# Attention with a constant column for the valid flags, and another order of GpSimd's large operations and of the first rearranging copies

## The chip, the cores and the metric

The kernel runs on one core of a Trainium2 chip. The metric is the device time of one execution in microseconds (us), the median of several runs; a profiled execution gives the trace from which all rows below are taken. Engines are named as in the profile: PE is TensorE's matmuls and PEld its weight loads, DVE is VectorE, ACT is ScalarE, POOL is GpSimd, SP is SyncE, which issues most of the DMAs.

## The reference, cut to what matters

```python
B, S, D, M, I = 32, 128, 512, 128, 2048
x = x + tanh(g_xattn[0]) * xattn(layernorm(x), ctx, mask)     # mask true: this key counts
x = x + tanh(g_ffn[0]) * ffn(layernorm(x), w_gate, w_up, w_down)

def xattn(h, mem, mask):
    scores = einsum('bsd,bmd->bsm', h, mem) / sqrt(D)
    scores = where(mask[:, None, :], scores, -1e30)
    readout = einsum('bsm,bmd->bsd', softmax(scores), mem)
    return where(any(mask, -1)[:, None, None], readout, 0)    # no valid key: nothing is added

def ffn(h, w_gate, w_up, w_down):
    h = silu(h @ w_gate) * (h @ w_up)
    return keep_2_largest_of_4(h) @ w_down
```

## The kernel before, in words

The work has two stages. The **attention stage** goes through the 32 batch rows b, each a tile of 128 tokens by 512, in 39 software-pipelined **slots** n (SLOTS = 32 + 7). Every engine runs its own loop over n in a fixed order, and in slot n it does different steps for different rows: PE transposes ctx and the normed x of row n-1, makes the scores of row n-2, transposes x1n of row n-7, multiplies probabilities by ctx for row n-4 and transposes the probabilities of row n-3. ACT copies the two transposes of row n-1, takes the exponential of row n-3, norms x of row n (xn), copies x1n's transpose of row n-7, and copies the transposed probabilities of row n-3 while it scales them. DVE's slot begins with the two small bn_aggr (L892 for row n-6, L896 for row n+1), and goes on with the masked scores (L909) and their minimum (L912) of row n-3, x1 of row n-5 (L924, attention plus residual), x1n of row n-6 (L930, the second layernorm, a tensor_scalar), and the bn_stats of x1 (L935, row n-5) and of x (L943, row n+2). POOL adds eps to the variances (L529), raises them and the softmax sum to their powers (L535, 128x3), and makes the shift of xn (L538, L542). DVE's x1n waits for that power, and POOL's addition waits for DVE's bn_aggr. In the text, the **start of slot n** is the start of L892 in it (for the first slots, L896).

Four kinds of work are laid into slots by hand, by the tables at the top of the file, for the feed-forward stage that follows:
- the mask: one DMA of 32 x 128 flags to all partitions, queued on SP behind the rows x and ctx of b = 0 and 1, with the two gates; POOL turns it into 0 or 1e30 (L548, four pieces of 1024, in slots 1, 2 and 3 by CONVERT), and DVE reduces it to one valid flag per row (L900, four operations), which with the gate scales the probabilities;
- the first weights: SP loads w_raw pieces (PIECE_AT, and two ahead of the slots), ACT rearranges them to w_blk ("spread", L290, SPREAD_AT), DVE makes sums of blocks (w_sum, SUM_AT), and ACT and POOL split each of 7 products' weights into a high and a low part (w_high on ACT, w_low L306 on POOL one slot later, W0_AT), which SP stores;
- the first x blocks, split in the same way (x_high on ACT, x_low L347 on POOL one slot later, X0_AT, 14 of them, with 8 DVE sums x_sum);
- in the last three slots PE already makes the first products of the feed-forward stage (product, L1231, L1233, L1235).

SP's loop loads x and ctx of row n+4 in slot n, once x1 of row n-5 is done (nine buffers each), stores x1 of row n-5, and stores 1 MB of transposed x1n every fourth slot. The order on DVE and on POOL around the change is (POOL's base, power and shift stand ahead of these lines):

```python
                if n in SUM_AT:
                    for u, i in SUM_AT[n]:
                        w_sum(dve, u, i)
                if n + 1 in X0_AT:
                    x_sum(dve, 0, *X0_AT[n + 1])
...
                if n - 1 in W0_AT:
                    w_low(pool, nc.gpsimd, 0, W0_AT[n - 1])
                if n - 1 in X0_AT:
                    x_low(pool, nc.gpsimd, 0, *X0_AT[n - 1])
```

The **feed-forward stage** runs 16 steps of two units of 14 products and 8 output tiles; it takes from the last slots to the end.

Of the kernel before, what the change touches and what calls it, by code (L numbers as in the profile page):

```python
# [5 lines left out]
F32 = mybir.dt.float32  # L6
# [24 lines left out]
BIG = 1e30  # L31
RING = 8
# [15 lines left out]
CONVERT = {1: (0,), 2: (1,), 3: (2, 3)}  # L48
# [52 lines left out]
def flamingo_gated(nc, x, ctx, mask, g_xattn, g_ffn, w_gate, w_up, w_down, out):  # L101
# [9 lines left out]
    with whole:  # L111
# [36 lines left out]
        neg_scores = sb("neg_scores", [P, 2, M], F32, 4)  # L148
# [9 lines left out]
        bn_mv = sb("bn_mv", [P, RING, 2, 2], F32, 4)  # L158
# [5 lines left out]
        eps = sb("eps", [P, 2], F32, 4)  # L164
# [3 lines left out]
        valid = sb("valid", [P, B], F32, 4)  # L168
        gate_valid = sb("gate_valid", [P, B], F32, 4)
        ident = sb("ident", [P, P], F32, 4)  # L170
        x_blk1 = sb("x_blk1", [P, 4, HALF], F32, 4)
        mask_in = x1nT[:, 0, 0:2].rearrange("p c n -> p (c n)").bitcast(U8)

# [29 lines left out]
        gates_loaded, mask_loaded, mask_neg_done = sem("gates_loaded"), sem("mask_loaded"), sem("mask_neg_done")  # L203
        neg_mean_done, shift_done = sem("neg_mean_done"), sem("shift_done")
        base_set = sem("base_set")
        ident_set, ident_done, half_done = sem("ident_set"), sem("ident_done"), sem("half_done")
        gates_done, valid_done, gate_valid_done = sem("gates_done"), sem("valid_done"), sem("gate_valid_done")
# [168 lines left out]
        def _(sp):  # L376
# [52 lines left out]
            load_w_piece(sp, nc.sync, 0, 0)  # L429
            load_w_piece(sp, nc.sync, 0, 1)  # L430
# [75 lines left out]
        def _(pool):  # L506
            nc.gpsimd.memset(base3[:], 1.0).then_inc(base_set, 1)
            nc.gpsimd.memset(eps[:], EPS)
            nc.gpsimd.memset(minus_one[:], -1.0)
            nc.gpsimd.memset(exponent3[:], -0.5).then_inc(half_done, 1)  # L510
            pool.wait_ge(half_done, 1)
            nc.gpsimd.memset(exponent3[:, 2:3], -1.0).then_inc(half_done, 1)
            nc.gpsimd.memset(ident[:], 0.0).then_inc(ident_set, 1)
# [3 lines left out]
            pool.wait_ge(half_done, 2)  # L517
            pool.wait_ge(base_set, 1)

            for n in range(-1, SLOTS - 1):  # L520
# [6 lines left out]
                if first or second:  # L527
                    part_v = slice(0 if first else 1, 2 if second else 1)
                    nc.gpsimd.tensor_tensor(base3[:, k, part_v], bn_mv[:, k, part_v, 1], eps[:, part_v],  # L529
                                            ALU.add).then_inc(base_done, 1)  # L530
                    pool.wait_ge(base_done, n + 2)
                if third:
                    pool.wait_ge(probs_done, n - 3)
                part_p = slice(0 if first else 1, 3 if third else 2 if second else 1)
                nc.gpsimd.tensor_tensor(power3[:, k, part_p], base3[:, k, part_p], exponent3[:, part_p],  # L535
                                        ALU.pow).then_inc(power_done, 1)
                if first:
                    nc.gpsimd.tensor_tensor(neg_mean[:, k:k + 1], bn_mv[:, k, 0, 0:1], minus_one[:],  # L538
# [4 lines left out]
                                            ALU.mult).then_inc(shift_done, 1)  # L543
                if n in CONVERT:
                    pool.wait_ge(mask_loaded, 16)
                    for at_m in CONVERT[n]:
                        part_m = slice(at_m * RING * M, (at_m + 1) * RING * M)
                        nc.gpsimd.tensor_scalar(mask_neg[:, part_m], mask_in[:, part_m], -BIG, BIG, ALU.mult,  # L548
                                                ALU.add).then_inc(mask_neg_done, 1)
# [43 lines left out]
        def _(act):  # L593
# [5 lines left out]
            for n in range(SLOTS):  # L599
# [8 lines left out]
                if 0 <= b < B:  # L608
                    act.wait_ge(neg_max_done, b + 1)
                    wait(act, pT_done, b - 1)  # L610
                    nc.scalar.activation(probs[:, b % 2], neg_scores[:, b % 2], ACT.Exp, bias=neg_max[:, b % RING:b % RING + 1],
                                         scale=-1.0, accum_out=base3[:, (b + 4) % RING, 2:3]).then_inc(probs_done, 1)
# [8 lines left out]
                if 0 <= b < B:  # L621
                    h = b // TILES
                    if b == 0:
                        act.wait_ge(mask_neg_done, 4)
                        act.wait_ge(valid_done, 4)
# [6 lines left out]
                    else:  # L632
                        if b % TILES == 0:
# [5 lines left out]
                if 0 <= b < B:  # L639
                    act.wait_ge(pT_done, b + 1)  # L640
                    wait(act, av_done, b - 1)
                    if b == 0:
                        act.wait_ge(gate_valid_done, 1)
                    nc.scalar.activation(probsT[:, b % 2], ps_pT[:, 0:P], ACT.Identity,
                                         scale=gate_valid[:, b:b + 1]).then_inc(pT_copied, 1)
                if n == 1:
# [240 lines left out]
        def _(dve):  # L887
            for n in range(-2, SLOTS):
                b = n - 6
                if 0 <= b < B:  # L890
                    dve.wait_ge(bn2_done, b + 1)
                    nc.vector.bn_aggr(bn_mv[:, n % RING, 1], bn6[:, 1, b % 2]).then_inc(stats2_done, 1)  # L892
# [443 lines left out]
```

## Time and profile before

| | us |
|---|---|
| median of 3 runs | 1117.73 (1117.38 to 1119.66) |
| the profiled execution | 1116.94 |
| its span, first to last instruction | 1115.1 |
| attention stage, to PE's first product | 134 |
| PE busy over the span | 1082.4 |

The profiled execution is 1.84 longer than its span and 0.79 shorter than the median. PE is busy 97% of the span, but in the attention stage PE's rows are overlapping short matmuls; there the time per slot has to be read from the starts of the slots and from the chain that ended last.

### The profile page before, as it was taken

How to read it: one execution, taken by the hardware profiler on the slowest of the kernel's cores; microseconds unless marked ns; L12 is line 12 of the kernel's file. 1: busy time of each engine (PE TensorE's matmuls, PEld its weight loads, DVE VectorE, ACT ScalarE, POOL GpSimd, SP SyncE). 2: the span in 40 equal slices, each digit the busy share in tenths (PEclk: the TensorE clock that was granted, in tenths of full speed). 3: DMA queues.
4: the chain of work that ended last, by engine and by line, in shares of the span. 5: the costliest groups of instructions: out<-in, count | busy, mean ns of one | idle time of the engine just before them, and what ended most of it. 6: DMA issues, size and time to landing. Idle time of an engine off the chain costs nothing.

```text
span 1115.1 us, 15146 instructions
## 1 busy us (share of the span) xinstructions
PE 1082.4 (97%) x4960; PEld 880.0 (79%) x4960; DVE 809.6 (73%) x1400; ACT 620.1 (56%) x1132; POOL 210.6 (19%) x328
## 2 busy tenths in 40 slices
PE   6998799999999999999999999999999999999998
PEld 5776587777878888888888888888888888888886
DVE  6999969879897757576775767675757565565765
ACT  5999678566765544454544444454445454443452
POOL 5576610121210111111111111001111111111111
PEclk9999999999999999999999999999999999999999
DMA  7899586798869977797779777888878666767726
GB/s 273 295 349 329 202 326 226 219 289 280 257 226 354 356 196 198 187 257 185 202 197 374 182 202 200 237 235 208 231 230 274 151 153 156 189 159 189 199 29 137
DMA packets 89533, 254.75 MB, mean 228 GB/s; under 512 B 9072, under 2 KB 9072, under 8 KB 85104
## 3 DMA queue, kind: packets, MB, share of 16 engines
q1 hardware_dynamic: 67856, 205.55, 52.2%
q0 software_dynamic: 21600, 48.24, 26.1%
q8 instruction: 40, 0.66, 0.2%
q14 instruction: 37, 0.30, 0.1%
HBM read 154.14 MB, written 99.61 MB: 228 GB/s over the span
## 4 chain that ended last, share of the span: by engine, by line
PE 73%; DVE 14%; ACT 4%; issue 4%; POOL 2%; DMA 2%; SPq 0%; DVEq 0%; ACTq 0%; POOLq 0%
PE ps_y L1302 9%; PE ps_a L1231 9%; PE ps_a L1233 9%; PE ps_a L1235 9%; PE ps_y L1304 9%; PE ps_y L1303 9%; PE ps_d L1233 4%; PE ps_d L1231 4%; PE ps_d L1235 4%; PE ps_c L1233 2%; PE ps_c L1231 2%; PE ps_c L1235 2%; DVE beats L980 2%; DMA w_raw<-in_L_ffn_w_up 1%; DVE x1n L930 1%
## 5 line engine op out<-in xcount | busy, mean ns | idle before, releaser
L569 POOL DMA_DIRECT2D out_rows<-y_out x124 | 107.1, 871 | 735.2 <-ACT y_out L717 712.7
L1231 PE MATMUL ps_a<-xm,w_ring 128*128 128x512 f32 x512 | 200.7, 392 | 3.6 <-ACT cp L597 3.3
L1233 PE MATMUL ps_a<-xm,w_ring 128*128 128x512 f32 x512 | 200.3, 391 | 0.0
L1235 PE MATMUL ps_a<-xm,w_ring 128*128 128x512 f32 x512 | 200.2, 391 | 0.0
L1302 PE MATMUL ps_y<-dn,h_hi 128*128 128x512 f32 x480 | 188.9, 394 | 4.4 <-ACT y_out L717 3.3
L1304 PE MATMUL ps_y<-dn,h_lo 128*128 128x512 f32 x480 | 187.4, 390 | 0.0
L1303 PE MATMUL ps_y<-dn,h_hi 128*128 128x512 f32 x480 | 187.0, 390 | 0.0
L717 ACT ACTIVATE y_out<-ps_y,ffn_gate 128x512 f32<-128x512 f32 x124 | 84.8, 686 | 158.4 <-PE ps_y L1304 158.3
L694 ACT ACTIVATE h_hi<-hidden 128x512 fp32r<-128x512 f32 x128 | 73.6, 626 | 107.0 <-DVE hidden L1006 107.0
L980 DVE TENSOR_TENSOR beats<-h_abs 128x512 bf16<-128x512 f32 x186 | 117.7, 684 | 1.3 <-ACT h_abs L687 1.3
L1231 PEld LDWEIGHTS ps_a<-xm,w_ring 128*128 128x128 f32 x512 | 96.4, 188 | 26.2 <-issue 5.2
L1235 PEld LDWEIGHTS ps_a<-xm,w_ring 128*128 128x128 f32 x512 | 96.5, 188 | 20.4
L1233 PEld LDWEIGHTS ps_a<-xm,w_ring 128*128 128x128 f32 x512 | 96.4, 188 | 20.0
L1302 PEld LDWEIGHTS ps_y<-dn,h_hi 128*128 128x128 f32 x480 | 90.1, 188 | 27.4 <-ACT y_out L717 7.4
L948 DVE TENSOR_TENSOR cp<-ps_c,cp 128x512 f32<-128x512 f32 x64 | 43.6, 689 | 93.7 <-PE ps_c L1235 93.7
L1304 PEld LDWEIGHTS ps_y<-dn,h_lo 128*128 128x128 f32 x480 | 90.1, 188 | 19.4
L1303 PEld LDWEIGHTS ps_y<-dn,h_hi 128*128 128x128 f32 x480 | 90.2, 188 | 18.7
L1231 PE MATMUL ps_d<-xm,w_ring 128*128 128x512 f32 x256 | 99.7, 390 | 0.5 <-ACT hidden L670 0.5
L1235 PE MATMUL ps_d<-xm,w_ring 128*128 128x512 f32 x256 | 99.6, 389 | 0.0
L1233 PE MATMUL ps_d<-xm,w_ring 128*128 128x512 f32 x256 | 99.6, 389 | 0.0
L954 DVE TENSOR_TENSOR hidden<-ps_a,hidden 128x512 f32<-128x512 f32 x64 | 43.8, 690 | 65.2 <-PE ps_a L1235 62.9
L687 ACT ACTIVATE h_abs<-hidden 128x512 f32<-128x512 f32 x124 | 74.1, 625 | 28.3 <-DVE hidden L972 28.3
(109 smaller groups left out, 1876.6 us busy)
## 6 DMA issues: line engine op xcount, KB each, us to landing
w_ring<-w_scratch SPq DMA_DIRECT2D x147, 512.0 KB, 4.5
out_rows<-y_out POOLq DMA_DIRECT2D x124, 256.0 KB, 4.3
w_scratch<-w_ring SPq DMA_DIRECT2D x56, 512.0 KB, 4.7
xm_scratch<-x_out SPq DMA_DIRECT2D x42, 512.0 KB, 5.4
xm<-xm_scratch SPq DMA_DIRECT2D x21, 1024.0 KB, 8.4
w_raw<-in_L_ffn_w_down SPq DMA_DIRECT2D x9, 1024.0 KB, 7.8
x_in<-in_x SPq DMA_DIRECT2D x32, 256.0 KB, 4.7
ctx_in<-in_ctx SPq DMA_DIRECT2D x32, 256.0 KB, 5.0
```

The lines of the kernel that those rows point to most:

```text
L569: nc.gpsimd.dma_start(out[RING * (n // (2 * TILES * QS)) + TILES * ORDER[order] + n % TILES], y_out[:, n % 4], accum_op=ALU.add).then_inc( ...
L687: nc.scalar.activation(abs_of(s, order)[:, j], hidden[:, h, j], ACT.Abs).then_inc(abs_done, 1)
L694: nc.scalar.activation(h_hi[:, h, j], hidden[:, h, j], ACT.Copy).then_inc(h_hi_done, 1)
L717: nc.scalar.activation(y_out[:, n % 4], ps_y[n % 2][:], ACT.Identity, scale=ffn_gate[:]).then_inc(y_copied, 1)
L954: nc.vector.tensor_tensor(hidden[:, 1, j], ps_a[e][:], hidden[:, 1, j], ALU.add).then_inc(c22_done[e], 1)
L980: nc.vector.tensor_tensor(beats[:, PAIR[i, j]], abs_of(s, order)[:, i], abs_of(s, order)[:, j], ALU.is_ge).then_inc(beats_done, 1)
L1231: nc.tensor.matmul(to, w_ring[:, k, e, 0, c], xm[:, k, 0, c], start=begins and c == 0, stop=False, skip_group_check=not begins)
L1233: nc.tensor.matmul(to, w_ring[:, k, e, 0, c], xm[:, k, 1, c], start=False, stop=False, skip_group_check=not begins)
L1235: last = nc.tensor.matmul(to, w_ring[:, k, e, 1, c], xm[:, k, 0, c], start=False, stop=c == 1, skip_group_check=not begins)
L1302: nc.tensor.matmul(to, h_hi[:, h, j, at], right[:, 0, j], start=at_j == 0, stop=False)
L1303: nc.tensor.matmul(to, h_hi[:, h, j, at], right[:, 1, j], start=False, stop=False)
L1304: last = nc.tensor.matmul(to, h_lo[:, h, j, at], right[:, 0, j], start=False, stop=at_j == GROUP - 1)
```

## The change

- The scores get one more column that is always FEW = 0.9e30. The minimum over 129 columns is then a real score if any key is valid, and 0.9e30 if none is, so that all exponentials are 0; the softmax sum gets LEAST = 1e-30 added before its reciprocal. DVE's four valid reduces (L900) and the product with the gate (L939) are gone, and ACT scales by the gate alone. The softmax sum is now written into `stats` beside the variances, and one POOL addition (base) covers all three values; it therefore waits for the exponential, as the power did.
- The mask comes in four DMAs: piece 0 and the gates behind the rows of b = 2, piece 1 behind b = 7, the others behind b = 8. The two weight pieces ahead of the slots go out behind b = 6. CONVERT has its four operations in slots 1, 5, 7 and 10.
- POOL waits for x1n of its slot before CONVERT, w_low and x_low.
- The tables move: spreads of unit 0 to slots 5, 6, 8 and 9 (were 3, 6, 9, 12), of unit 1 to 19, 20, 35, 36 (20, 23, 26, 29); sums one per slot in 11 to 14 and 37, 38 (13 twice, 14, 15, 30 twice); loads to match; x_high from 21 to 34 without a gap (19 to 25 and 29 to 35), x_low one slot later, and x_sum in the slot of x_high, not one ahead: slots 24 to 27 and 31 to 34 (were 21 to 24 and 31 to 34).
- The two tanh are in slot 2 of ACT (were slot 1), and ACT's wait for the mask pieces in slot 23 (was 7).

```diff
-CONVERT = {1: (0,), 2: (1,), 3: (2, 3)}
+CONVERT = {1: 0, 5: 1, 7: 2, 10: 3}
...
-PIECE_AT = {4: (0, 2), 7: (0, 3), 10: (1, 0), 13: (1, 1), 21: (1, 2), 24: (1, 3), 27: (2, 0), 30: (2, 1)}
-SPREAD_AT = {3: (0, 0), 6: (0, 1), 9: (0, 2), 12: (0, 3), 20: (1, 0), 23: (1, 1), 26: (1, 2), 29: (1, 3)}
-SUM_AT = {13: ((0, 0), (0, 1)), 14: ((0, 2),), 15: ((0, 3),), 30: ((1, 0), (1, 1))}
-W0_AT = {5: 0, 8: 1, 14: 2, 15: 3, 16: 4, 17: 5, 18: 6}
-X0_AT = {19 + i: (0, i) for i in range(7)} | {29 + i: (1, i) for i in range(7)}
+PIECE_AT = {6: (0, 2), 7: (0, 3), 10: (1, 0), 11: (1, 1), 20: (1, 2), 21: (1, 3), 36: (2, 0), 37: (2, 1)}
+SPREAD_AT = {5: (0, 0), 6: (0, 1), 8: (0, 2), 9: (0, 3), 19: (1, 0), 20: (1, 1), 35: (1, 2), 36: (1, 3)}
+SUM_AT = {11: (0, 0), 12: (0, 1), 13: (0, 2), 14: (0, 3), 37: (1, 0), 38: (1, 1)}
+W0_AT = {7: 0, 10: 1, 14: 2, 15: 3, 16: 4, 17: 5, 18: 6}
+X0_AT = {21 + i: (0, i) for i in range(7)} | {28 + i: (1, i) for i in range(7)}
...
+            def load_mask(m):
+                at_m = slice(m * GROUP_M, (m + 1) * GROUP_M)
+                sp.dma_start(mask_in[:, at_m], mask.rearrange("b m -> (b m)")[at_m].rearrange("(a n) -> a n", a=1)
+                             .to_broadcast([P, GROUP_M])).then_inc(mask_loaded[m], 16)
...
-                if b == 1:
-                    sp.dma_start(mask_in, mask.rearrange("b m -> (b m)").rearrange("(a n) -> a n", a=1)
-                                 .to_broadcast([P, B * M])).then_inc(mask_loaded, 16)
+                if b == 6:
+                    load_w_piece(sp, nc.sync, 0, 0)
+                    load_w_piece(sp, nc.sync, 0, 1)
+                if b == 7:
+                    load_mask(1)
+                if b == 2:
+                    load_mask(0)
...
+            nc.gpsimd.memset(neg_scores[:, :, M:M + 1], FEW).then_inc(few_set, 1)
...
-                if first or second:
-                    part_v = slice(0 if first else 1, 2 if second else 1)
-                    nc.gpsimd.tensor_tensor(base3[:, k, part_v], bn_mv[:, k, part_v, 1], eps[:, part_v],
-                                            ALU.add).then_inc(base_done, 1)
-                    pool.wait_ge(base_done, n + 2)
+                part_p = slice(0 if first else 1, 3 if third else 2 if second else 1)
                 if third:
                     pool.wait_ge(probs_done, n - 3)
-                part_p = slice(0 if first else 1, 3 if third else 2 if second else 1)
+                nc.gpsimd.tensor_tensor(base3[:, k, part_p], stats[:, k, part_p, 1], least[:, part_p],
+                                        ALU.add).then_inc(base_done, 1)
+                pool.wait_ge(base_done, n + 2)
...
+                if second:
+                    pool.wait_ge(x1n_done, n - 5)
                 if n in CONVERT:
...
-                if n in CONVERT:
-                    dve.wait_ge(mask_loaded, 16)
-                    for m in CONVERT[n]:
-                        nc.vector.tensor_reduce(valid[:, m * RING:(m + 1) * RING],
...
-                    nc.vector.scalar_tensor_tensor(neg_scores[:, b % 2], ps_sc[b % 2][:, 0:M], -SCALE,
+                    nc.vector.scalar_tensor_tensor(neg_scores[:, b % 2, 0:M], ps_sc[b % 2][:, 0:M], -SCALE,
                                                    mask_neg[:, b * M:b * M + M], ALU.mult, ALU.add).then_inc(neg_scores_done, 1)
+                    if b == 0:
+                        dve.wait_ge(few_set, 1)
...
-                if n + 1 in X0_AT:
-                    x_sum(dve, 0, *X0_AT[n + 1])
+                if n in X0_AT:
+                    x_sum(dve, 0, *X0_AT[n])
```

## Rows read from the trace of the kernel before

**Rows 1.** The page: busy time, share of the span and instructions of each engine.
```profile
PE 1082.4 (97%) x4960; PEld 880.0 (79%) x4960; DVE 809.6 (73%) x1400; ACT 620.1 (56%) x1132; POOL 210.6 (19%) x328
```

**Rows 2.** Windows: stretch, length, busy time by engine (count), PE clock, DMA share, GB/s.
```profile
28.64:48.19 19.55, 19.30 (x138) 15.66 (x138) 18.67 (x49) 19.55 (x50) 11.20 (x26) 1.00 0.97 339
...
78.60:96.89 18.29, 15.62 (x103) 11.31 (x102) 18.15 (x37) 16.75 (x37) 10.68 (x21) 1.00 0.95 355
...
134.16:174.00 39.84, 39.84 (x182) 32.96 (x183) 29.44 (x47) 29.84 (x50) 6.48 (x10) 1.00 0.86 322
```

**Rows 3.** The chain that ended last, attention stage: start, length, what.
```profile
80.58 1.45 DVE x1n L930
...
119.04 1.25 POOL xm L347
...
134.16 0.66 PE ps_d L1266 x4
```

**Rows 4.** One line's instructions, L930: duration in ns, min/median/max.
```profile
L930 DVE TENSOR_SCALAR x1n<-x,bn_mv,power x32: 535/546/1550, 27.0 to 139.2; 128x512 f32<-128x512 f32 x32
```

**Rows 5.** The same view for L943.
```profile
L943 DVE BATCH_NORM_STATS2 bn<-x_in x32: 669/676/694, 3.5 to 112.6; 128x6 f32<-128x512 f32 x32
```

**Rows 6.** Timeline, slots 20 and 21, POOL's large operations: start, length, engine, line.
```profile
77.49 1.27 POOL L347 TENSOR_TENSOR xm<-x_blk,xm 128x512 fp32r<-128x512 f32 x1
...
80.48 1.27 POOL L347 TENSOR_TENSOR xm<-x_blk,xm 128x512 fp32r<-128x512 f32 x1
```

**Rows 7.** Timeline of DVE: starts of slots 13 to 16, and the first sum.
```profile
48.19 0.16 DVE L892 BATCH_NORM_AGGREGATE bn_mv<-bn 128x2 f32<-128x6 f32 x1
...
50.43 0.69 DVE L312 TENSOR_TENSOR w_blk<-w_blk 128x512 f32<-128x512 f32 x1 [1.43 <-ACT w_blk L290]
...
54.08 0.16 DVE L892 BATCH_NORM_AGGREGATE bn_mv<-bn 128x2 f32<-128x6 f32 x1
...
57.71 0.16 DVE L892 BATCH_NORM_AGGREGATE bn_mv<-bn 128x2 f32<-128x6 f32 x1
...
62.26 0.16 DVE L892 BATCH_NORM_AGGREGATE bn_mv<-bn 128x2 f32<-128x6 f32 x1
```

**Rows 8.** Timeline of DVE: starts of slots 30 to 32, x1n of slot 31.
```profile
113.22 0.17 DVE L892 BATCH_NORM_AGGREGATE bn_mv<-bn 128x2 f32<-128x6 f32 x1
...
117.82 0.18 DVE L892 BATCH_NORM_AGGREGATE bn_mv<-bn 128x2 f32<-128x6 f32 x1
...
119.69 0.89 DVE L930 TENSOR_SCALAR x1n<-x,bn_mv,power 128x512 f32<-128x512 f32 x1
...
121.22 0.18 DVE L892 BATCH_NORM_AGGREGATE bn_mv<-bn 128x2 f32<-128x6 f32 x1
```

**Rows 9.** Timeline, first 29 us; in brackets the idle time before and its releaser.
```profile
10.48 0.69 DVE L943 BATCH_NORM_STATS2 bn<-x_in 128x6 f32<-128x512 f32 x1 [3.37 <-DMA x_in<-in_x]
...
14.59 1.91 PE L1258 MATMUL ps_c<-ctxT,xnT 128*128 128x128 f32 x8
...
15.15 2.31 DVE L900 TENSOR_REDUCE valid<-x1nT 128x8 f32<-128x1024 uint8 x2
...
17.38 0.28 DVE L909 SCALAR_TENSOR_TENSOR neg_scores<-ps_c,mask_neg 128x128 f32<-128x128 f32 x1
...
20.57 1.12 ACT L290 ACTIVATE w_blk<-w_raw 128x512 f32<-128x512 f32 x1 [1.11 <-DMA w_raw<-in_L_ffn_w_gate]
...
28.64 0.17 DVE L892 BATCH_NORM_AGGREGATE bn_mv<-bn 128x2 f32<-128x6 f32 x1
```

**Rows 10.** Timeline: ACT's exponential of slot 10, DVE's x1 of slot 12.
```profile
41.45 0.55 ACT L611 ACTIVATE probs<-neg_scores,neg_max 128x128 f32<-128x128 f32 x1
...
45.79 0.75 DVE L924 SCALAR_TENSOR_TENSOR x<-ps_y,power,x_in 128x512 f32<-128x512 f32 x1
```

**Rows 11.** DMA issues from 73.6 to 74.5: KB each, us to landing.
```profile
x_in<-in_x SPq DMA_DIRECT2D x1, 256.0 KB, 7.1
```

**Rows 12.** Windows, 70 to 90 us, columns as in the second group.
```profile
70.00:90.00 20.00, 18.26 (x124) 13.56 (x123) 19.43 (x45) 18.93 (x45) 14.91 (x29) 1.00 1.03 391
```

More of the change, by code:

```diff
@@ L31 @@
 BIG = 1e30
+FEW = 0.9e30
+LEAST = 1e-30
 RING = 8
@@ L202, in flamingo_gated @@
         ctx_in_loaded = [sem(f"ctx_in_loaded{k}") for k in range(INPUTS)]
-        gates_loaded, mask_loaded, mask_neg_done = sem("gates_loaded"), sem("mask_loaded"), sem("mask_neg_done")
+        gates_loaded, mask_neg_done = sem("gates_loaded"), sem("mask_neg_done")
+        mask_loaded = [sem(f"mask_loaded{k}") for k in range(B // RING)]
         neg_mean_done, shift_done = sem("neg_mean_done"), sem("shift_done")
-        base_set = sem("base_set")
+        stats_set, few_set = sem("stats_set"), sem("few_set")
         ident_set, ident_done, half_done = sem("ident_set"), sem("ident_done"), sem("half_done")
-        gates_done, valid_done, gate_valid_done = sem("gates_done"), sem("valid_done"), sem("gate_valid_done")
+        gates_done = sem("gates_done")
         bn1_done, stats1_done, bn2_done, stats2_done = (
@@ L543, in _ @@
                                             ALU.mult).then_inc(shift_done, 1)
+                if second:
+                    pool.wait_ge(x1n_done, n - 5)
                 if n in CONVERT:
[L545 to L549, printed above, removed]
+                    m = CONVERT[n]
+                    pool.wait_ge(mask_loaded[m], 16)
+                    part_m = slice(m * GROUP_M, (m + 1) * GROUP_M)
+                    nc.gpsimd.tensor_scalar(mask_neg[:, part_m], mask_in[:, part_m], -BIG, BIG, ALU.mult,
+                                            ALU.add).then_inc(mask_neg_done, 1)
                 if n - 1 in W0_AT:
@@ L610, in _ @@
                     wait(act, pT_done, b - 1)
[L611 to L612 removed]
+                    nc.scalar.activation(probs[:, b % 2], neg_scores[:, b % 2, 0:M], ACT.Exp, bias=neg_max[:, b % RING:b % RING + 1],
+                                         scale=-1.0, accum_out=stats[:, (b + 4) % RING, 2, 1:2]).then_inc(probs_done, 1)
                 b = n
@@ L887, in _ @@
         def _(dve):
+            dve.wait_ge(stats_set, 1)
             for n in range(-2, SLOTS):
@@ L891, in _ @@
                     dve.wait_ge(bn2_done, b + 1)
-                    nc.vector.bn_aggr(bn_mv[:, n % RING, 1], bn6[:, 1, b % 2]).then_inc(stats2_done, 1)
+                    nc.vector.bn_aggr(stats[:, n % RING, 1], bn6[:, 1, b % 2]).then_inc(stats2_done, 1)
                 b = n + 1
@@ L914, in _ @@
                 if n in SUM_AT:
-                    for u, i in SUM_AT[n]:
-                        w_sum(dve, u, i)
-                if n + 1 in X0_AT:
-                    x_sum(dve, 0, *X0_AT[n + 1])
+                    w_sum(dve, *SUM_AT[n])
+                if n in X0_AT:
+                    x_sum(dve, 0, *X0_AT[n])
                 b = n - 5
@@ L929, in _ @@
                     dve.wait_ge(power_done, n + 2)
-                    nc.vector.tensor_scalar(x1n[:, b % 2], x1[:, b % 4], bn_mv[:, n % RING, 1, 0:1],
+                    nc.vector.tensor_scalar(x1n[:, b % 2], x1[:, b % 4], stats[:, n % RING, 1, 0:1],
                                             power3[:, n % RING, 1:2], ALU.subtract, ALU.mult).then_inc(x1n_done, 1)
```

47 lines of the change are left out of this document (19 added, 28 removed).

## Prediction

> **What bounds the kernel now.** I read the page first: PE is busy 97% of the span [rows 1], which says little about the attention stage, where the change is. The windows show the border between two regimes. From 134.16 to 174.00 PE is busy 39.84 of 39.84 us; between 78.60 and 96.89 DVE is busy 18.15 of 18.29 and PE idles 2.7; between 28.64 and 48.19 ACT is busy all of 19.55 [rows 2]. So the attention stage is set by DVE, with ACT at the limit early on, and the feed-forward stage by PE. The chain that ended last says the same. It runs through DVE's x1n slot after slot, through POOL's x_low late in the stage, and passes to PE at 134.16, where four transposes wait for x1n of slot 35 and the first product follows at once [rows 3]. Whatever x1n of slot 35 gains, PE starts earlier by, and PE has no hole before 174 that could take it back.
>
> Next I read x1n alone: 0.546 at the median of 32, 1.55 at most, while bn_stats never leaves 0.669 to 0.694 [rows 4, 5]. The timeline gives the reason. In slot 21 POOL's x_low runs from 80.48 to 81.75; x1n starts at 80.58 and ends at 82.03, 0.28 after x_low is over [rows 3, 6]. In slot 20 x_low starts at 77.49, when x1n is already past, and bn_stats under it keeps its length [rows 5, 6]. So a large POOL operation in progress holds x1n until it ends, and costs 0.90 there; beside bn_stats it costs nothing.
>
> Then the length of a slot. Slots 16 to 20 take from 62.26 to 78.60 [rows 2, 7], 16.34/5 = 3.27 each, a **normal slot**. A slot with one DVE sum and no collision is slot 14: 57.71 - 54.08 = 3.63 [rows 7]. The sum of 0.69 costs only 0.36, since x1n of a normal slot waits for POOL's power anyway. With a collision (slot 15) it is 62.26 - 57.71 = 4.55 [rows 7], so the collision costs 0.92.
>
> **The change part by part.**
>
> *Start, slots -1 to 6.* The third row of x is waited for until 10.48, 3.37 idle, behind the 512 KB mask and the two gates; then four valid reduces take 1.1 to 1.2 each, the last two until 17.46, and the first masked scores come at 17.38, though they need only the first scores and mask piece 0 [rows 9]. Afterwards x of row 2 is queued ahead of the mask. The reduces are gone, and the first masked scores can run in DVE's slot 3 at about 12.9: 4.5 earlier. Not all of this lasts. The early matmuls are slow (1.91 for the eight of one row's scores at 14.59 [rows 9]), so PE and ACT become the chain of slots 3 to 5. Walking through the order of PE and ACT with these durations, I get the exponential of slot 3 at 14.6 and that of slot 5 at 21.2 (20.2 if PE is fast from 14 us on, 22.5 if it is slow until 18). ACT's first spread waited 1.11 for its DMA at 20.57 [rows 9]; in slot 5 it finds its data. The start of slot 7 moves from 28.64 [rows 9] to about 25.0: **-3.6** (-2.2 to -4.4).
>
> *Slots 7 to 15.* Before: 62.26 - 28.64 = 33.62 [rows 7, 9]. In it slot 13 takes 5.89: two sums, and 1.43 idle for the spread of slot 12, in which ACT is late [rows 7]. Afterwards there are five normal slots and four sum slots without collision: 5 x 3.27 + 4 x 3.63 = 30.87. ACT has to keep up. x1 of slot n comes no earlier than the exponential of slot n-2 plus 45.79 - 41.45 = 4.34, read where this just bound [rows 10]. From 28.64 to 48.19 ACT does the work of six slots, two spreads (1.12 each [rows 9], some 1.03 where the next operation overlaps) and one w_high (about 0.5): 19.55 = 6a + 2.6 [rows 2], so a plain ACT slot is 2.8, one with a spread 3.85, one with a w_high 3.35. From 21.2 this gives exponentials of slots 9, 10 and 11 at about 35.0, 38.9 and 42.2, so x1 of slots 11, 12 and 13 at 39.4, 43.2 and 46.6 at the earliest; DVE alone would have them at 39.4, 43.1 and 46.7. The two tie, and I add 0.2. The stretch gets 31.1: **-2.5** (-1.5 to -3). POOL's conversions in slots 5, 7 and 10 end before the next slot's addition.
>
> *Slots 16 to 29.* The sums move from slots 21 to 24 to 24 to 27. Before, the four took 18.29 [rows 2]; without collision 4 x 3.63 = 14.52: **-3.8**. The wait for x1n puts x_low at about 2.6 into the slot, over at 3.9, when the next addition is wanted; nothing else is queued on POOL, and power follows in time. In normal slots x_low started after x1n already, so the wait is free. If POOL's start after x1n were late by 0.3, it would cost 0.3 in some ten slots; that is the upper bound, and nothing is the lower.
>
> *Slots 30 to 35.* Slot 30 took 4.60 (117.82 - 113.22) [rows 8], with two sums and a collision. The sums are moved to slots 37 and 38, where x1n waits for power and PE is busy with products. What is left is bn_aggr to x1, power, x1n at 1.5, its end at 2.05, one bn_stats: 2.75, **-1.85**. Slots 31 to 34 took 3.40 each (121.22 - 117.82), x1n in them 0.89 [rows 8]; at 0.55 they take 3.07: **-1.35** for four. Here POOL is close to being the next bound: x_low 1.27, addition and power about 1.1, x1n 0.55, with the gaps 3.05. In slot 35 x1n loses its collision (0.9) but waits 0.5 longer for power, since x_low of slot 34 is now ahead of it: **-0.35**.
>
> *Costs.* The column adds one element of 129 to the minimum: nothing measurable. The wider addition is under the exponential's wait, which ended long before in all but the first slots. Spreads of slots 19 and 20 put ACT 1.1 later in its slot; the reading above allows an exponential 2.9 after the slot's start, and I get 2.5. The loads in slots 36 and 37 are wanted by ACT about 12 later. The large risk is **DMA**. A load of x issued in slot 19 took 7.1 to land [rows 11], and if slots are normal it is needed 7.7 after its issue: from x1 in slot n to bn_stats in slot n+2 are two slots and 1.1. Slots 15 to 22 now issue, in 8 x 3.27 = 26.2 us, 8 x 0.79 MB of rows, five stores of 0.52, two pieces of 0.52 and two stores of 1.05: 12.1 MB, at the 391 GB/s of a full window [rows 12] 30.9 us. The queue falls behind by 4.7, about what the prefetch allows (7.7 less some 3 for an unhindered load, as the first one, which is there for L943 at 3.5 [rows 5]). Lumps will show: I take **+1.2**, between nothing and 3.5.
>
> By the Trainium skill, DMA: Bandwidth & Descriptors, section Bandwidth, a core's HBM traffic is bound at about 358 GB/s. That would make 33.7 us of the 12.1 MB and a stall of about 2.8. The 391 GB/s over 20 us is above that figure, and I go by the row [rows 12].
>
> **The sum.** -3.6 - 2.5 - 3.8 - 1.85 - 1.35 - 0.35 + 1.2 = -12.25. The profiled execution's 1116.94 becomes 1104.7; the median of the runs is 0.79 above it, so 1105.5.
>
> **The rivals.**
> - *DMA becomes the bound of slots 20 to 26.* For: the 7.1 us load, and windows at 1.03 share [rows 11, 12]. Against: the slots that made that backlog are the same as before. x waits add up to 3.5 to 5 in place of 1.2: 1108 to 1109.5.
> - *ACT holds the early slots.* For: ACT fully busy from 28.64 to 48.19 [rows 2]; two pairs of spreads now stand in adjacent slots. If the chain starts 2 later or each slot costs 0.3 more, slots -1 to 15 give 2.5 to 3.5 in place of 6.1: 1108 to 1109.5.
> - *Collisions with two-input operations.* In slots 31 to 34 x_low ends 0.7 into the next slot, and the sum starts at 0.6. If sums were held as x1n is, four slots grow by 0.15 and slots 25 to 28 a little: about +0.7, 1106.2. No row shows a sum under a large POOL operation. The Trainium skill, GPSIMD Engine Reference, section Key points, counts operations with two SBUF inputs among those that contend with GpSimd.
> - *Slower: POOL becomes the bound.* Its 24 large operations wait for x1n in order, and addition and power, for which the next x1n waits, stand behind them. From a late start of 12.25/24 = 0.5 per slot beyond the slack the change only costs; at 0.7 it gives 1122. POOL's slack in a normal slot is 0.2, but no row shows so late a start after DVE's signal.
> - *The gain is given back* in the feed-forward stage, in whose first steps loads move later: 1117. Against it is PE without a hole to 174 [rows 2].
>
> **How the numbers follow.** The forecast, 1103 to 1107.5, gets 0.63; DMA 0.14; ACT 0.10; two-input collisions 0.05; POOL 0.03; given back 0.03; the remaining 0.02 is a larger gain than I see. The range 1102.0 to 1109.0 takes the forecast, the collisions and most of the first two rivals, 8 in 10 or a little over. 0.2% (2.2 us) is about what a measurement of this kernel can tell from no change. The first three rivals stay faster, so faster has 0.93, the same 0.04, slower 0.03.
>
> **What would show it.** x1n never above 0.6 in slots with a sum. Sum slots of 3.63, slots 31 to 34 of 3.07, slot 30 of 2.75. First masked scores near 13, start of slot 7 near 25 and of slot 16 near 56.1; PE's first product near 122. Idle time of bn_stats L943 for DMA around slots 19 to 25, of 0 to 2 in sum. From there on the same times as before. What would make it wrong: x waits beyond 3, x1 waiting for PE in slots 8 to 13, POOL's addition late against bn_aggr in most slots, or a feed-forward stage longer than before.

## The result and the profile after

The changed kernel takes 1109.49 us (median of 7 runs, 1107.79 to 1113.76) beside 1118.96 for the kernel before on the same chip (7 runs, 1117.38 to 1119.91): ratio 0.992, 95% interval 0.9904 to 0.9935. It is faster, as forecast, but 4.0 above the predicted 1105.5 and 0.5 above the range. The profiled execution took 1110.76, with a span of 1108.7.

The page, busy time by engine (answers to [rows 1]). DVE works 12.6 less, since the reduces are gone and x1n is shorter; PE has as many instructions as before.

```profile
PE 1079.8 (97%) x4960; PEld 877.2 (79%) x4960; DVE 797.0 (72%) x1395; ACT 620.6 (56%) x1132; POOL 214.8 (19%) x330
```

The windows, columns as in [rows 2]: slots 7 to 12, slots 24 to 27 (the sum slots, which were 21 to 24), slots 30 to 34, and 39.84 from PE's first transpose of x1n of slot 35. The first window now has two sums in it.

```profile
23.83:44.62 20.79, 20.10 (x138) 15.10 (x137) 19.61 (x51) 20.79 (x53) 14.07 (x28) 1.00 0.95 323
83.51:98.52 15.01, 14.30 (x96) 10.34 (x95) 14.54 (x37) 13.87 (x33) 10.45 (x20) 1.00 0.99 373
105.06:121.52 16.46, 13.44 (x84) 9.28 (x84) 14.88 (x37) 13.02 (x34) 12.88 (x18) 1.00 0.38 142
123.87:163.71 39.84, 39.84 (x182) 33.04 (x183) 29.71 (x49) 30.92 (x51) 6.77 (x10) 1.00 0.96 352
```

The sum slots 24 to 27 now take 15.01 (18.29 for 21 to 24 before), ACT is busy in all of slots 7 to 12, and PE is still without a hole for 39.84. But in the third window no engine is full: DVE 14.88 of 16.46, POOL 12.88. Something waits there in a circle. The chain that ended last names it (start, length, what; answers to [rows 3]):

```profile
80.93 9.66 DMA x_in<-in_x
90.61 0.69 DVE bn L948
...
107.31 1.28 POOL xm L351
108.58 0.63 POOL base L543
109.29 0.70 POOL power L546
109.99 0.70 issue
110.72 1.28 POOL xm L351
...
123.27 0.56 DVE x1n L939
123.87 0.66 PE ps_d L1271 x4
```

From slot 30 on the chain is POOL's, slot after slot: x_low (L351), addition, power, DVE's x1n behind the power ("issue"), and x_low again. PE takes over at 123.9 (134.16 before). Ahead of that stands a load of x that took 9.66.

Grouped by line, x1n (L939, was L930) and bn_stats of x (L948, was L943); these answer to [rows 4] and [rows 5]. The last row is the idle time ahead of L948 and its number of times.

```profile
L939 DVE TENSOR_SCALAR x1n<-x,stats,power x32: 540/546/548, 22.2 to 128.8; 128x512 f32<-128x512 f32 x32
...
L948 DVE BATCH_NORM_STATS2 bn<-x_in x32: 674/682/695, 3.6 to 104.5; 128x6 f32<-128x512 f32 x32
...
  DMA x_in<-in_x: 9.9, 7
```

The collision of x1n is gone altogether: 548 ns at most, where it was 1550. Next the timeline of the changed kernel at five places, starting with the first slots (answers to [rows 9]), then slot 13 ([rows 7]), slots 23 and 25 ([rows 11]) and slot 31 ([rows 8]).

```profile
10.63 0.69 DVE L948 BATCH_NORM_STATS2 bn<-x_in 128x6 f32<-128x512 f32 x1 [2.40 <-DMA x_in<-in_x]
...
12.36 1.06 PE L1263 MATMUL ps_c<-ctxT,xnT 128*128 128x128 f32 x8
12.82 0.28 DVE L917 SCALAR_TENSOR_TENSOR neg_scores<-ps_c,mask_neg 128x128 f32<-128x128 f32 x1
...
19.88 1.05 POOL L562 TENSOR_SCALAR mask_neg<-x1nT 128x1024 bf16<-128x1024 uint8 x1 [1.73 <-DMA x1nT<-in_mask_BxS_bk]
...
22.17 0.55 DVE L939 TENSOR_SCALAR x1n<-x,stats,power 128x512 f32<-128x512 f32 x1 [1.33 <-POOL power L546]
...
23.83 0.17 DVE L906 BATCH_NORM_AGGREGATE stats<-bn 128x2 f32<-128x6 f32 x1
...
45.34 1.42 POOL L546 TENSOR_TENSOR power<-base,exponent 128x3 f32<-128x3 f32 x1
45.36 0.68 DVE L323 TENSOR_TENSOR w_blk<-w_blk 128x512 f32<-128x512 f32 x1
...
82.90 0.69 DVE L948 BATCH_NORM_STATS2 bn<-x_in 128x6 f32<-128x512 f32 x1 [1.24 <-DMA x_in<-in_x]
...
90.61 0.69 DVE L948 BATCH_NORM_STATS2 bn<-x_in 128x6 f32<-128x512 f32 x1 [0.34 <-DMA x_in<-in_x]
...
111.89 0.68 DVE L361 TENSOR_TENSOR x_blk<-x_blk 128x512 f32<-128x512 f32 x1
111.95 0.67 POOL L543 TENSOR_TENSOR base<-stats,least 128x2 f32<-128x2 f32 x1
...
112.70 0.70 POOL L546 TENSOR_TENSOR power<-base,exponent 128x2 f32<-128x2 f32 x1
...
113.50 0.55 DVE L939 TENSOR_SCALAR x1n<-x,stats,power 128x512 f32<-128x512 f32 x1 [0.27 <-POOL power L546]
```

The first masked scores are at 12.82 (17.38 before), and the eight matmuls of one row's scores take 1.06 already at 12.36, where at 14.59 before they took 1.91. Above all the reader is to see the pair at 111.89 and 111.95. DVE's sum starts first, POOL's addition of a few numbers 0.06 later, and that addition takes 0.67 where it takes 0.20 elsewhere: it ends at 112.62, just behind the sum (112.57). Power and x1n come later by as much. In slot 13 the power is stretched in the same way, 1.42 beside 0.85, though its record starts 0.02 ahead of the sum's.

Term by term, from the starts of the slots in both traces (the term's name is the prediction's):

| term | predicted | measured |
|---|---|---|
| start of slot 7 | -3.6 | 23.83 - 28.64 = -4.8 |
| slots 7 to 15 | -2.5 | 31.91 - 33.62 = -1.7 |
| slots 16 to 29, with DMA | -3.8 + 1.2 = -2.6 | 49.32 - 50.96 = -1.6 |
| slot 30 | -1.85 | 2.80 - 4.59 = -1.8 |
| slots 31 to 34 | -1.35 | 13.66 - 13.56 = +0.1 |
| slot 35 to the end of x1n | -0.35 | 2.29 - 2.74 = -0.45 |
| sum | -12.25 | -10.3 |

So 1.95 of the 4.0 was lost in the attention stage. Another 1.2 is not the change's: the kernel before has a median of 1118.96 here and had 1117.73 in the runs shown. The last 0.8 is the difference between 10.3 gained at x1n and 9.5 gained at the medians; it goes in the feed-forward stage (below).

### The profile page after: what moved, and what is told of

Read it like the earlier page. It is cut to its first block, busy times and chain, and to the rows that moved or that the text cites. A ratio compares the mean times of both kernels' runs of the same rounds, so it can differ in the third digit from the quotient of the medians.

```text
span 1108.7 us, 15154 instructions
## 1 busy us (share of the span) xinstructions
PE 1079.8 (97%) x4960; PEld 877.2 (79%) x4960; DVE 797.0 (72%) x1395; ACT 620.6 (56%) x1132; POOL 214.8 (19%) x330
## 4 chain that ended last, share of the span: by engine, by line
PE 76%; DVE 10%; DMA 5%; ACT 3%; issue 3%; POOL 1%; SPq 1%; DVEq 0%; ACTq 0%; POOLq 0%
PE ps_a L1236 9%; PE ps_a L1238 9%; PE ps_a L1240 9%; PE ps_y L1307 9%; PE ps_y L1309 8%; PE ps_y L1308 8%; PE ps_d L1236 4%; PE ps_d L1238 4%; PE ps_d L1240 4%; PE ps_c L1236 2%; PE ps_c L1240 2%; PE ps_c L1238 2%; DMA x_blk<-xnT_scratch 2%; DMA w_raw<-in_L_ffn_w_up 2%; DVE beats L985 1%
```

## Experiments

Each is the changed kernel with one edit unless it says otherwise. The ratios are to the kernel before, whose median beside them was 1118.4 to 1118.8.

### Without POOL's wait for x1n

```diff
-                if second:
-                    pool.wait_ge(x1n_done, n - 5)
```

> The changed kernel without POOL's wait for x1n before its large operations; all else stays. Theory A (the wait is worth what it removes of collisions, and POOL's large operations hold x1n): x1n is 1.4 to 1.5 again in slots 24 to 27, these slots take 4.5 in place of 3.63 to 4.1, slots 31 to 34 stay near 3.4, slot 35 and 36 get some 0.4 longer; the execution is 3.5 to 4.5 us longer than the changed kernel, about 1113.5 or 0.995 of the kernel before. Rival B (the gain comes from the order of the sums and loads alone, the wait only shifts work): within 1 us of the changed kernel, 0.992.

Measured: 1112.28 (1111.18 to 1113.52), ratio 0.9945 (0.993 to 0.996). Slots 24 to 27 take 4.55 each, x1n of slot 35 ends at 127.36, 3.55 later than with the wait; the median is 2.8 higher, less than the 3.5 to 4.5 expected. The timeline of slot 24: x_low starts 0.11 ahead of x1n, and x1n lasts until 0.29 after it.

```profile
84.78 1.27 POOL L351 TENSOR_TENSOR xm<-x_blk,xm 128x512 fp32r<-128x512 f32 x1
...
84.89 1.45 DVE L937 TENSOR_SCALAR x1n<-x,stats,power 128x512 f32<-128x512 f32 x1
```

### The wait alone, in the kernel before

```diff
+                if second:
+                    pool.wait_ge(x1n_done, n - 5)
                 if n in CONVERT:
```

> The kernel before with one line more, POOL's wait for x1n. Theory A: x1n back at 0.55 in slots 15, 21 to 24, 30, 35 and 36; slots 21 to 24 take 3.63 and slot 15 too; slots 31 to 34 stay at 3.4, since POOL's addition now falls under DVE's sum and is held by it. Sum about -5.5 us, 0.995. Rival B (nothing holds POOL's addition): slots 31 to 34 take 3.07, sum about -7. Rival C (the wait makes POOL late): 0 or slower.

Measured: 1114.75 (1111.92 to 1115.91), ratio 0.9965 (0.9952 to 0.9977); x1n of slot 35 ends at 129.65, 4.5 earlier than before. x1n is 0.55 everywhere, the four sum slots take 3.64 instead of 4.55, and slots 31 to 34 3.29 to 3.40. Slot 14 takes 3.88 instead of 3.63, and slot 15 takes 3.88 and not the 3.63 expected: in both, power starts 0.02 ahead of the sum and takes 1.41. The two kernels together: at x1n of slot 35 the wait is worth 4.5 alone and 3.6 within the change, of the 10.3 that the whole change gained there.

### The sum ahead of x1n instead of ahead of x1

```diff
-                if n in SUM_AT:
-                    w_sum(dve, *SUM_AT[n])
-                if n in X0_AT:
-                    x_sum(dve, 0, *X0_AT[n])
                 b = n - 5
                 ...
+                if n in SUM_AT:
+                    w_sum(dve, *SUM_AT[n])
+                if n in X0_AT:
+                    x_sum(dve, 0, *X0_AT[n])
                 b = n - 6
```

> The changed kernel with DVE's sum of a slot between x1 and x1n, not ahead of x1. Theory A (a DVE sum with two SBUF inputs holds a POOL operation that starts under it; this is why slots 31 to 34 take 3.41 and not 3.07, and slots 13 and 14 3.89 and not 3.63): POOL's addition is back at 0.19 and its power at 0.70 to 0.86 in these slots, which take 3.1 and 3.64; 1.5 to 2 us less than the changed kernel, about 1107.7. Rival B (slots 31 to 34 are at the bound of POOL's own chain x_low, addition, power, x1n): slots 31 to 34 stay at 3.4, no change of the time.

Measured: 1105.79 (1105.01 to 1106.92), ratio 0.9887 (0.9873 to 0.9902). Slots 31 to 34 take 3.05, 13 and 14 take 3.64, and x1n of slot 35 ends at 121.71, 2.1 earlier than in the change. In its timeline of slot 31 the addition lasts 0.20 again; the sum comes after it, while power is running, and keeps its 0.68:

```profile
107.90 0.20 POOL L543 TENSOR_TENSOR base<-stats,least 128x2 f32<-128x2 f32 x1
108.18 0.69 POOL L546 TENSOR_TENSOR power<-base,exponent 128x2 f32<-128x2 f32 x1
108.49 0.68 DVE L358 TENSOR_TENSOR x_blk<-x_blk 128x512 f32<-128x512 f32 x1
109.09 0.54 DVE L939 TENSOR_SCALAR x1n<-x,stats,power 128x512 f32<-128x512 f32 x1
```

The addition is shorter by 0.47 and the slot by 0.36, for x1n now stands behind the sum on DVE: it starts 0.22 behind the end of power, where it was 0.10 (113.50 beside 112.70 + 0.70). So the stretched addition was what slots 31 to 34 lost, and a bound of 3.4 in POOL's chain of itself is refuted. In slots 24 to 27 it is now POOL's neg_mean that starts under the sum and takes 0.65 to 0.68 instead of 0.19; nothing waits for it there, and sum slots without a wait for x keep their 3.64. By the medians this kernel is 3.7 faster than the change; 2.1 of that is gained at x1n, and the other 1.6 lies behind it, in the feed-forward stage, which the edit doesn't touch and in which one kernel's traces differ by 0.8 to 1.1 (the second traces below).

### The sum behind x1n, under x_low

The same four lines between x1n and the bn_stats of x1.

> The changed kernel with DVE's sum of a slot right behind x1n, so that it starts at the moment at which POOL's large operation wants to start. Theory A (two-input sum and large POOL operation exclude each other, whoever is first): in slots 24 to 27 and 31 to 34 either x_low lasts 1.8 to 1.9 or the sum 1.3 to 1.9, each of these slots 4.0 to 4.5 and 3.6 to 4.0; 3 to 5 us more than the changed kernel. Rival B (only x1n's kind of operation is held, two-input sums run beside a large POOL operation): sum 0.69 and x_low 1.27 in these slots, which take 3.9 and 3.1; within 1 us of the changed kernel.

Measured: 1108.51 (1107.32 to 1111.84), ratio 0.9921 (0.99 to 0.9942), x1n of slot 35 ends at 123.73: no better than the change. Of the two victims that my first theory left open it is x_low, and the price was too high: 3 to 5 more were expected, and the time is within 1, as the rival said for another reason. The timeline of slot 31:

```profile
110.39 0.69 DVE L358 TENSOR_TENSOR x_blk<-x_blk 128x512 f32<-128x512 f32 x1
110.56 1.65 POOL L351 TENSOR_TENSOR xm<-x_blk,xm 128x512 fp32r<-128x512 f32 x1 [0.74 <-DVE x1n L935]
```

The sum is first and keeps 0.69; x_low, which has two inputs in the same memory as the sum, takes 1.65 instead of 1.27. It holds up what stands behind it on POOL: 3.87 to 4.01 for slots 24 to 27 and 3.3 to 3.5 for 31 to 34.

### The sum ahead of x1n, and two weight pieces loaded later

```diff
-..., 20: (1, 2), 21: (1, 3), 36: (2, 0), 37: (2, 1)}
+..., 28: (1, 2), 29: (1, 3), 36: (2, 0), 37: (2, 1)}
```

> The changed kernel with the sum between x1 and x1n, and the loads of weight pieces (1, 2) and (1, 3), whose data are wanted in slots 35 and 36, in slots 28 and 29 and not 20 and 21. Theory A (the idle time of bn_stats for x in slots 21 to 25, 0.8 to 1.8 us, comes from these 1 MB being in the DMA queue with the stores of xnT and w): the waits for x after slot 20 vanish, slots 21 to 25 take 3.3, 3.3, 3.3, 3.64, 3.64, and the time is 0.8 to 1.5 below that of the same kernel without this edit, about 1104.7. Rival B (the waits come from stores and row loads alone): they stay, no change, 1105.8.

Measured: 1106.17 (1104.11 to 1107.84), ratio 0.9883 (0.9863 to 0.9902). Slots 21 to 25 take 3.33, 3.33, 3.58, 3.64 and 3.64. The waits of bn_stats for x come to 0.21, all in slot 23. With the same order of the sum and the early loads they came to 0.85: 0.14 in slot 21, 0.28 in slot 23 and 0.43 in slot 25. So slot 25's wait is gone with the 1 MB that was queued among the rows (in the kernel with all three edits too), and slot 23's is not. x1n of slot 35 ends at 121.31, only 0.4 earlier, since slots 10 and 11 took 3.82 and 3.91 in this execution; the time is the same as without the edit, and the 0.8 to 1.5 expected did not come.

### The sum ahead of x1n, and mask piece 1 converted in slot 6

```diff
-CONVERT = {1: 0, 5: 1, 7: 2, 10: 3}
+CONVERT = {1: 0, 6: 1, 7: 2, 10: 3}
```

> The changed kernel with the sum between x1 and x1n, and POOL's conversion of mask piece 1 in slot 6 and not 5. Theory A (in slot 5 POOL stands 1.7 us in front of a mask piece that has not landed, and everything behind it, addition, power and x1n of slot 6, is late by that): slot 6 takes 3.3 in place of 4.45, the idle 1.3 of x1n there goes; 0.8 to 1.2 less at the start of slot 16, about 1104.8. Rival B (ACT with its spreads in slots 5, 6, 8, 9 sets the start of slot 16 anyway): slot 6 is shorter and slots 7 to 12 longer by the same, no change at slot 16.

Measured: 1107.04 (1106.02 to 1108.91), ratio 0.9894 (0.9878 to 0.991). Slot 6 takes 3.20 instead of 4.46, and slots 10 and 11 take 3.81 and 3.90 instead of 3.33 and 3.66. Slot 16 starts at 55.80, where it was 55.78. What holds slot 10 is seen on POOL: its addition waits for ACT's exponential, as the merged addition has to, and starts 0.62 behind DVE's bn_aggr. In slot 11 it is 0.71.

```profile
34.76 0.20 POOL L543 TENSOR_TENSOR base<-stats,least 128x3 f32<-128x3 f32 x1 [1.98 <-ACT probs L625]
```

So POOL's wait for mask piece 1 costs nothing in the end: ACT sets the start of slot 16, and DVE waits for it in slot 6 or in slots 10 and 11. x1n of slot 35 ends at 122.26, 0.55 later than without the edit, since bn_stats waits 0.5 longer for x in slots 21 to 25.

### The column alone

The kernel before with the column, the merged addition and the mask in four DMAs behind b = 1; no wait for x1n, all six tables as before. The four valid reduces are gone.

> The kernel before with the constant column alone: no valid reduces, one addition for all three bases, but the mask queued behind b = 1, all tables, and POOL's order as before (the mask comes in four DMAs in place of one). Theory A (the start gains because DVE loses the four reduces and the wait for them, but ACT and the spread in slots 3 and 12 take part of it back): start of slot 7 at 26 to 27.5 in place of 28.6, start of slot 16 1 to 3 earlier, the rest as before; 1116 to 1117. Rival B (the reduces were hidden behind the DMAs): nothing, 1118.5.

Measured: 1121.71 (1120.24 to 1123.03), ratio 1.0027 (1.0017 to 1.0037): slower than before. The first masked scores come at 14.09, 3.3 earlier than before, and yet slot 7 starts at 30.96, 2.3 later. Its timeline of ACT and DVE, and its windows of four us (PE's granted clock is the third number from the end):

```profile
20.71 1.11 ACT L294 ACTIVATE w_blk<-w_raw 128x512 f32<-128x512 f32 x1 [4.25 <-DMA w_raw<-in_L_ffn_w_gate]
...
25.20 1.91 PE L1258 MATMUL ps_c<-ctxT,xnT 128*128 128x128 f32 x8
...
27.21 0.29 DVE L911 SCALAR_TENSOR_TENSOR neg_scores<-ps_c,mask_neg 128x128 f32<-128x128 f32 x1 [3.66 <-PE ps_c L1258]
```
```profile
16.00:20.00 4.00, 2.66 (x17) 1.63 (x15) 1.44 (x5) 0.45 (x2) 3.60 (x7) 1.00 1.06 388
20.00:24.00 4.00, 0.78 (x4) 0.78 (x5) 2.25 (x5) 3.29 (x7) 2.03 (x7) 0.66 0.30 97
24.00:28.00 4.00, 4.00 (x17) 3.46 (x16) 0.58 (x2) 2.41 (x6) 2.05 (x7) 0.50 0.88 272
```

ACT reaches its first spread in slot 3 earlier than before, and the weights still land at 20.7; it stands for 4.25, where it stood 1.11 [rows 9]. Behind it everything waits. PE idles 4.56, and its granted clock falls to 0.50 (the level of 1.2 GHz) until 28: the scores of the next row take 1.91 for eight matmuls at 25.20, where the eight that stood at 24.29 in the kernel before took 1.06. The time saved ahead of a fixed landing is lost, and the slow matmuls behind the pause cost about 2.2 more: from one transposition of probabilities to the next, with the same matmuls in between, PE takes 5.14 (from 23.22 to 28.36), where the kernel before took 2.95 (from 23.10 to 26.05).

### The column with the tables of the first 18 slots

The kernel above with the change's spreads, loads, conversions and sums up to slot 18; from slot 19 on as before, and no wait for x1n.

> The column-only kernel (all old tables) started slot 7 at 30.96, 2.3 later than before, because ACT stood 4.25 in the spread of slot 3 and POOL's addition now waits for the exponential behind it. Here the tables of the first 18 slots are the change's (first spreads in slots 5, 6, 8, 9, their loads, CONVERT 1, 5, 7, 10, sums 11 to 14, w_high 7 and 10); everything from slot 19 on is as before, no wait for x1n, four mask DMAs behind b = 1. Theory A (the column only pays with the spreads behind slot 4): start of slot 7 at 23.8 to 24.5, start of slot 16 at 55.5 to 57, x1n of slot 35 ends near 128, 1112 to 1114, ratio 0.995. Rival B (the column itself delays the start through POOL's merged addition, whatever the spreads): start of slot 7 at 27 or later, 1116 to 1119.

Measured: 1112.91 (median of 9, eight from 1111.31 to 1115.32 and one of 1201.43), ratio 0.9947 (0.9931 to 0.9964). Slot 7 starts at 24.01 and slot 16 at 56.45, and PE's granted clock is 1.00 in each window from 12 to 24. So with both nearly all of the 4.8 at the start is there (4.6), and with the column alone none of it: the column frees DVE, and the spreads in slots 5 and 6 keep ACT from standing in front of the weights' landing. What these tables give without the column was not run.

### The mask's DMAs first, as before

All four mask DMAs and the gates behind b = 1, the first weight pieces behind b = 8.

> The changed kernel with the four mask DMAs and the gates behind b = 1 and the two weight pieces behind b = 8, as in the kernel before. Theory A (x of row 2 waits for the mask in the queue, and the first slots are set by the arrival of x): first masked scores about 1 us later, at 13.9; start of slot 7 0.5 to 1.5 later unless POOL's wait for mask piece 1 in slot 5, which goes with this edit, gives 1.2 back: then the start of slot 7 is within 0.5 of the changed kernel. Rival B (the order of the DMAs does all of the start's gain): start of slot 7 2 or more later, +2 us.

Measured: 1109.37 (1107.54 to 1111.0), ratio 0.9912 (0.9895 to 0.993): the time of the change. Slot 7 starts at 23.98, slot 6 takes 3.21, slots 10 and 11 take 3.83 and 4.19, slot 16 starts at 56.95. The order of these DMAs is worth nothing that can be measured.

### All three edits together

The sum ahead of x1n, the late pieces and the conversion in slot 6.

> The kernel with the sum between x1 and x1n, with pieces (1,2) and (1,3) loaded in slots 28 and 29 and CONVERT in 1, 6, 7, 10. Theory A (each removes a wait, but slots 10 and 11 take it back through ACT): x1n of slot 35 ends at 121.3 to 122.3, 1105 to 1107, not to be told from 1105.8. Rival B (the two add up, since the late loads leave the bandwidth to x while slot 6 is short): x1n of slot 35 ends at 120.5, 1104.

Measured: 1105.73 (1104.29 to 1107.13), ratio 0.9878 (0.9848 to 0.9907), beside 1105.79 for the sum's move alone. In its profiled execution x1n of slot 35 ended at 120.66, but no gain in time beyond the one edit can be told. Of the three edits only the sum's place is worth something in time.

### The change and the kernel before once more

Both unchanged, one execution each, for second traces.

> The change once more, for a second profile. Theory A (what the feed-forward stage gave back, 2.1 at unit 4 and 1.9 at unit 8, is the chance of DMA landings): x1n of slot 35 ends again at 123.8 within 0.4, while the loss from there to the end differs from 3.9 by 1 or more. Rival B (it is a collision of the earlier stage with its loads): 3.9 again, within 0.4, at the same units.

> The kernel before once more, for a second profile. Theory A (chance of landings in the feed-forward stage): x1n of slot 35 ends at 134.1 within 0.4 and the span is 0.5 to 3 longer than 1115.1, all of it between units 4 and 8. Rival B: 1115.1 again within 0.4.

Measured: the change 1109.69 with a span of 1107.7, x1n of slot 35 ending at 123.94; the kernel before 1117.79 with a span of 1116.0, x1n ending at 134.17. The attention stage repeats within 0.13. Behind it the change, which had given back 3.8 against the first trace of the kernel before, some 2 each at units 4 and 8, now gives back 2.7, with 1.2 of it at unit 4; the kernel before loses 0.8 at unit 4 that it hadn't lost. Both are in the sense of the first theory, though the losses come at the same two places. What happens at unit 4 is a wait of PE and then its clock. PE's first product of the output tiles there, in the kernel before, in the change, and in the change again:

```profile
237.51 0.50 PE L1302 MATMUL ps_y<-dn,h_hi 128*128 128x512 f32 x1 [1.84 <-ACT y_out L717]
```
```profile
228.37 0.50 PE L1307 MATMUL ps_y<-dn,h_hi 128*128 128x512 f32 x1 [3.01 <-ACT y_out L730]
```
```profile
227.59 0.50 PE L1307 MATMUL ps_y<-dn,h_hi 128*128 128x512 f32 x1 [2.10 <-ACT y_out L730]
```

And the window of 5 us around or behind that wait, in the kernel before and in the kernel before again (235 to 240), and in the change (230 to 235):

```profile
235.00:240.00 5.00, 3.16 (x14) 2.26 (x14) 4.67 (x8) 4.20 (x7) 2.57 (x3) 1.00 0.89 288
```
```profile
235.00:240.00 5.00, 3.22 (x12) 2.28 (x11) 4.48 (x8) 4.25 (x7) 2.57 (x3) 0.87 0.87 288
```
```profile
230.00:235.00 5.00, 5.00 (x18) 3.99 (x17) 4.96 (x10) 1.87 (x4) 1.33 (x2) 0.72 0.97 185
```

The same kernel, with PE waiting 1.84 in one execution and 1.78 in the other, is granted 1.00 in one and 0.87 in the other, and loses 0.8. The change waited 3.01, because ACT stood for two weight loads ahead of y_out (4.43 and 2.81), and was granted 0.72 afterwards. The variants spread in the same way: with the sum ahead of x1n PE waited 1.92 there and was granted 1.00, and the loss from x1n to the end was 0.1; with the conversion in slot 6 as well it waited 3.15, was granted 0.58 from 225 to 230, and the loss was 3.5. No edit of these two touches that stage.

## Why the prediction was right or wrong

**Right: the direction and the main terms.** x1n is never above 0.55, a sum slot is 3.64, slot 30 is 2.80, slot 35 gains 0.45. The kernels with and without the wait show that the wait does it, and that POOL isn't hurt by it in normal slots (3.27 as before). POOL's chain did become the bound of slots 31 to 34, but the rival that it makes the kernel slower did not come.

**Wrong: slots 31 to 34 (-1.35 predicted, +0.1 measured).** This is the largest miss. What failed is the step that costed the sum at nothing for POOL. The prediction gave DVE's slot 3.07 and POOL's cycle 3.05 with its gaps. With the sum moved away from the addition these slots do take 3.05, but it is DVE that fills them (busy 11.91 of 12.18); POOL's cycle by itself is shorter, 2.93 in slot 35, which has no sum. That the two numbers meet is luck. The rival "collisions with two-input operations" named the place, but had the sum as the victim and 0.15 per slot as the price. The victim is POOL's operation that starts just behind the sum, and since the cycle runs through it, its 0.47 costs 0.36 per slot. The Trainium skill, SBUF — State Buffer, section Who interferes with whom, says that a DVE tensor_tensor with both inputs in SBUF contends with GpSimd's reads, that the pair of ports they share is an exclusive lock, and that the order of issue decides who is held. By that rule the addition runs behind the sum's end at 112.57 and is over at 112.76, and x_low behind the sum's end at 111.08 is over at 112.35; the traces show 112.62 and 112.21, both 0.14 earlier, so they agree but for that. In the other direction the traces don't show it for the sum: at 111.89 it starts 0.11 before x_low is over (110.72 + 1.28), and with the sum moved, at 108.49, in the middle of power, and it stays at 0.68 both times. No run has a sum that starts well inside a large POOL operation. x1n behind a running x_low is the case in which DVE is held.

**Slots 7 to 15 (-2.5 predicted, -1.7 measured).** 0.5 of the 0.8 is the same effect: in slots 13 and 14 POOL's power starts 0.02 ahead of the sum and takes 1.42; they last 3.89 instead of the 3.63 counted, and 3.64 once the sum is moved. In the kernel without the wait, power starts 0.08 ahead of the sum in slot 13 and is not stretched, so the collision hangs on a few hundredths. Slot 7 is 0.35 longer than the normal slot counted: POOL's addition starts 0.50 behind bn_aggr there, and x1n stands 0.49 for power. In the other kernels with the change's tables and the wait it is 0.48 to 0.57, with the wait taken out 0.08, and the slot is 3.23; why the wait makes the addition late in this slot alone is open. The rest of the reasoning, that ACT and DVE tie here, holds: whatever was gained in slot 6 came back as waits in slots 10 and 11. It came back through the merged addition, whose wait for the exponential the prediction took to be over long before in all but the first slots.

**Slots 16 to 29 (-3.8 and +1.2).** The collisions' -3.8 is right: 14.52 was counted for the sum slots, and they take 15.01, which is that and slot 25's wait for x. Of the DMA term, bn_stats waited in slots 23 and 25 (1.24 and 0.34), which are 1.34 and 0.45 too long: 1.8 where 1.2 was taken, inside its bounds of 0 and 3.5. The same kernel once more waited 0.86 and 0.35, so a part is scatter. With two pieces loaded later the waits come to 0.21 and 0.22 in two kernels, where the five traces with the early loads and the sum ahead of x1 or of x1n, all with the wait for x1n, have 0.8 to 1.6. That fits the cause named, the queue behind x; two traces don't prove it, since the kernel with the sum behind x1n waited only 0.07 with the early loads. The remaining 0.3 are hundredths in slots 20 to 22 and 27.

**The start (-3.6 predicted, -4.8 measured).** The mechanism was right, and a size was off: the term for slots -1 to 6 was too small by 1.2. The prediction took PE's early matmuls to stay at 1.91 for a while, and the exponential of slot 5 at 21.2, or 20.2 with PE fast from 14 on. PE was fast from 12 on, and the exponential came at 18.80. Part of this was taken back by a wait that the prediction denied, POOL's 1.73 for mask piece 1 in slot 5; the later slots showed that it costs nothing in the end. What the prediction did not say is that the column by itself would make the kernel slower. It counted ACT's wait for the first spread as 1.11 removed by the new tables, and not that with the old ones ACT arrives 3.0 earlier at the same landing.

**The feed-forward stage.** The prediction took PE to carry 10 to 12 us through unharmed. At x1n 10.3 was gained, and 6.5 was left in the first pair of profiles, 7.5 and 8.3 if the change's second profile is compared with the first and the second of before; by the medians it was 9.5. What is shown is that the two places, unit 4 and unit 8, lose different amounts in executions of the same kernel, also in the kernel before. Whether the change makes such a loss there more likely was not settled: among the change and its variants the loss from x1n to the end ran from 0.1 to 3.8.

## What to carry to other kernels

A small operation of GpSimd can be as dear as a large one: look at what DVE starts in the tenth of a microsecond ahead of it, and place DVE's two-input operations where no GpSimd operation that others wait for starts under them. When work ahead of an engine's DMA wait is made faster, move the wait too, or the gain ends at the landing and the pause behind it costs TensorE its clock. An idle slot at one engine is worth removing only if the next slots aren't set by another one; the start of a later slot shows it, not the length of the repaired one.

## What the runs showed of the hardware that was not expected

- A few hundredths decide whether GpSimd is held by DVE's sum: in all eight cases in which power's record starts 0.02 ahead of the sum's it took 1.41 or 1.42; with 0.05 to 0.13 ahead it took 0.85 or 0.86.
- An operation of GpSimd that starts under the sum ends at a fixed distance behind the sum's end, whenever it started: 0.05 for the addition, whether it started 0.06 or 0.26 behind the sum's start, and 1.13 or 1.14 for x_low. Each is its usual duration less 0.14 or 0.15.
- A GpSimd operation on 128x2 elements took 0.67 instead of 0.20, and one on 128x512 took 1.65 instead of 1.27, beside a DVE sum that kept its 0.68 to 0.69.
- With waits of 1.84 and 1.78 at the same place in two executions of one kernel, TensorE was granted 1.00 and 0.87. After 4.56 without work it was granted 0.50 until 28 in the kernel with the column alone.
- In the first 16 us the granted clock doesn't tell here how fast TensorE is: in the windows from 12 to 16 it is 1.00 in both kernels, and the eight matmuls of one row's scores take 1.91 at 14.59 in the one and 1.06 at 15.27 in the other.
